# Score tiles of 64 keys by two heads, one exponential a tile, and single-bank pieces in two flat cross attentions

## The chip, the cores and the metric

The kernel runs on one core of one Trainium2 chip. The metric is the device time of one launch in microseconds; less is better. Three runs of the kernel before gave 6174.67, 6178.66 and 6187.05 us; the median, 6178.66, is the time before.

## What is computed

A decoder of four layers for 1024 tokens of width 128; every layer has a self attention, a cross attention and a feed-forward part. The change touches the cross attentions of layers L1 and L2, which attend over the whole context of 6404 rows with 16 heads of 8 values. Both are plain softmax attentions; L1 has a mask of queries by keys, L2 one of keys alone and biases.

```python
# L1_xattn (L2_xattn: q, kv with bias, mask[:, None, None, :] -> -inf)
scores = einsum('bhqd,bhkd->bhqk', Q, K) / sqrt(d_k)        # 16 heads, 1024 queries, 6404 keys
scores = where(mask[:, None] == 0, -1e9, scores)
attn = softmax(scores, axis=-1)
Z = einsum('bhqk,bhkd->bhqd', attn, V)
out = Z @ Wo + bo
```

## The kernel before, in words

`P` is 128, `BANK` 512 (one PSUM bank of float32), `KT` 51 key tiles of 128, `NT` 8 query tiles. Both attentions call `context_sides` (L1090) and then `cross` (L1262), `masked_attention` (L1559) with `mask8` and `maskT`, `cross_attention` (L1661) without.

`context_sides` makes keys and values of all heads from the turned context in 13 groups of up to four key tiles. TensorE makes the products, ScalarE copies the keys twice, VectorE and GpSimd (L1167, L1169) split them into three bfloat16 parts, and VectorE copies the values into `vall` (L1156, or L1159 with a bias), 8 values and a one for every head and tile; GpSimd first sets the ones (L1163). SP stores the parts after every group, and the values at three groups (L1181), as rows of `values_dram`.

`cross` works on pairs of heads (8) and halves of the queries (2 x 512), 16 halves `h` in all. A head's split keys and queries lie in 64 of the 128 partitions (`SLOT`), head `a` of the pair in half `a`. For each half there are three kinds of work:

- **Pieces** (L1382 to L1391, VectorE L1500 to L1520) find the maximum score of each query: 49 rows, 128 queries, 512 keys, for both heads into two neighbouring banks. A half has 4 query tiles by 13 key chunks, 52 pieces. VectorE takes the maximum, masked by a custom operation for each head with the mask bytes subtracted (L1515), unmasked by one reduce over both banks (L1510). The banks form a ring of two places of two banks (4 to 7), which also carries the turning of queries (`queries`, L1391 on), the turning of the shifted queries (`shifted`) and the sums (`add_up`).
- **Scores** (L1411 to L1427): 128 keys by 512 queries of one head into one of three banks (0 to 2), with three more rows that subtract the maximum. Masked, two products of `lower` with `maskT` (L1418) first put the mask into the banks. ScalarE makes the exponential of each bank (L1480).
- **Weighing** (L1429 to L1446): every two key tiles, four products of 9 columns (values and the one) with 512 queries in float32, each in its own 32 columns of the array, summed in bank 3. After a half the sums are folded over the key tiles by `fold` and divided on VectorE.

The order is written out by hand in `programme` (L1233): one list of steps that TensorE, ScalarE and VectorE all follow. The pieces of half `h + 1` are spread between the scores of half `h` (`spread`, `cut`), so that the maxima are there when the half begins; `LEAD` pieces go one half further ahead. Weighing comes three tiles behind its scores (`lag`). TensorE's queue is in order: `ring_wait` before a piece waits until VectorE has freed the place, and a score waits for the exponential that reads its bank (`probs_ready`). SP loads the keys and values of a pair while the pair before it is worked on.

## Time and profile before

| | |
|---|---|
| median of three runs | 6178.66 us |
| lowest, highest | 6174.67, 6187.05 us |
| profiled execution, first to last instruction | 6180.5 us |
| TensorE, VectorE, ScalarE, GpSimd busy | 4319.4, 3667.5, 2628.5, 756.9 us |
| exponentials (L1480) | 3264, 1734.3 us busy, 598 ns each |
| weighing (L1441) | 6528 instructions, 873.0 us busy |
| masked maxima (L1515) | 1664 custom instructions, 1049.1 us busy |
| unmasked maxima (L1510) | 832 reduces, 956.2 us busy |

The table is from the page of the profile, whose times come from one execution on the chip. The only time of that execution that is given is its span, 6180.5 us, which lies between the median and the highest of the three runs. Busy is a union over the instructions of a group, so products that run beside each other count once. A float32 product is two instructions in the profile. Ends of matrix products are modelled; their starts are safer to compare.

### The profile page before, as it was taken

The numbers are of one execution on the slowest core, as the hardware profiler recorded it, in microseconds if no ns is written. First come the engines' busy times: TensorE is split into PE (matmuls) and PEld (weight loads), VectorE is DVE, ScalarE is ACT, GpSimd is POOL, SyncE is SP. The second block draws the span as 40 slices with busy tenths as digits, with TensorE's granted clock in tenths as the row PEclk, the third lists the DMA queues.
The fourth block names the chain that finished last, engine by engine and source line by source line (L and its number), as shares of the span: only waits on it lengthen the run. The fifth ranks groups of instructions, "written<-read, shape, count | busy, mean of one in ns | idle before, by whom it ended". The sixth has DMA issues, their size and how long they took to land. (4 is left out here: it accounts for less than half of the span.)

```text
span 6180.5 us, 82959 instructions
## 1 busy us (share of the span) xinstructions
PE 4319.4 (70%) x31970; PEld 1559.0 (25%) x31970; DVE 3667.5 (59%) x7693; ACT 2628.5 (43%) x4771; POOL 756.9 (12%) x842
## 2 busy tenths in 40 slices
PE   5956999544699999999964899999877641134224
PEld 2333444333122222222242122222134320012011
DVE  5464666556877777777345998998724650137122
ACT  2522666224366666666611587888730110001001
POOL 0000000002000000000002000000000027722772
PEclk9878999767799999999976899999988875567567
DMA  0020000024000000000004001100014000000000
GB/s 13 1 62 10 15 11 9 15 100 155 18 12 10 3 12 12 12 12 1 1 6 104 1 12 19 17 12 12 1 15 147 13 5 13 12 5 5 13 13 8
DMA packets 119874, 141.87 MB, mean 23 GB/s; under 512 B 48269, under 2 KB 96620, under 8 KB 116846
## 3 DMA queue, kind: packets, MB, share of 16 engines
q1 hardware_dynamic: 77870, 118.15, 7.6%
q0 software_dynamic: 20480, 10.53, 1.1%
q10 hardware_dynamic: 21128, 7.88, 0.5%
q8 instruction: 253, 4.15, 0.3%
q14 instruction: 143, 1.17, 0.1%
HBM read 103.35 MB, written 33.14 MB: 22 GB/s over the span
## 5 line engine op out<-in xcount | busy, mean ns | idle before, releaser
L1480 ACT ACTIVATE probs<-ps 128x512 f32<-128x512 f32 x3264 | 1734.3, 598 | 763.0 <-PE ps L1425 762.9
L1515 DVE CUSTOM_DVE_ANT_0 junk<-ps,mask 128x512 bf16<-128x512 f32 (+1 forms) x1664 | 1049.1, 678 | 362.5 <-PE ps L1387 346.4
L1510 DVE TENSOR_REDUCE maxima<-ps 128x2 f32<-128x1024 f32 (+1 forms) x832 | 956.2, 1199 | 110.6 <-PE ps L1387 104.2
L1441 PE MATMUL ps<-probs,vstack 128*9 128x512 f32 x6528 | 873.0, 596 | 0.4 <-ACT probs L1480 0.4
L1425 PE MATMUL ps<-qturned,kturned 52*128 52x512 bf16 x3264 | 792.8, 385 | 83.7 <-ACT probs L1480 64.8
L1387 PE MATMUL ps<-kturned,qturned 49*128 49x512 bf16 (+1 forms) x3328 | 704.6, 392 | 110.8 <-DVE maxima L1510 35.7
L3172 POOL DMA_INDIRECT line<-table,index x640 | 644.8, 1008 | 876.9 <-DVE index L3545 483.5
L1418 PE MATMUL ps<-maskT,lower 128*128 128x512 fp8e5 x1632 | 562.3, 387 | 63.5 <-ACT probs L1480 15.1
L1425 PEld LDWEIGHTS ps<-qturned,kturned 52*128 52x128 bf16 x3264 | 196.2, 93 | 791.8 <-ACT probs L1480 462.1
L1387 PEld LDWEIGHTS ps<-kturned,qturned 49*128 49x128 bf16 x3328 | 166.3, 95 | 492.7 <-DVE maxima L1510 200.3
L1418 PEld LDWEIGHTS ps<-maskT,lower 128*128 128x128 bf16 x1632 | 123.5, 96 | 598.6 <-ACT probs L1480 433.4
L2733 PE MATMUL ps<-plane,bands 32*32 32x512 f32 x6720 | 249.7, 608 | 17.6 <-DVE top L2885 17.6
L1163 POOL MEMSET vall<- 128x816 f32 x2 | 3.1, 1569 | 2041.0 <-POOLq L66 2041.0
L2831 ACT COPY powerT<-ps 128x512 f32<-128x512 f32 x280 | 164.2, 586 | 203.5 <-PE ps L2747 203.3
L3299 PE MATMUL ps<-ident,attended 128*128 128x128 f32 x8 | 3.8, 475 | 340.0 <-DVE attended L3569 198.1
L2875 DVE SCALAR_TENSOR_TENSOR plane<-keep,ps 128x1024 f32<-128x1024 uint8 x144 | 175.7, 1220 | 102.4 <-PE ps L2715 102.4
L2823 ACT ACTIVATE power<-power,bias 128x512 f32<-128x512 f32 x280 | 202.5, 725 | 56.2 <-DVE bias L2893 56.2
L2747 PE MATMUL ps<-ident,power 128*128 128x128 f32 x1120 | 183.0, 286 | 32.4 <-ACT powerT L2831 31.4
L2885 DVE CUSTOM_DVE_ANT_0 power<-ps,lose 128x512 f32<-128x512 f32 x280 | 176.8, 687 | 41.7 <-PE ps L2733 41.7
L3608 DVE SCALAR_TENSOR_TENSOR siluT<-ps,hash_b,yT 128x512 f32<-128x512 f32 x16 | 12.0, 752 | 314.5 <-DMA rows<-in_ctx 242.8
L3230 PE MATMUL ps<-prod,vpar 128*128 128x512 f32 x128 | 70.9, 683 | 138.7 <-issue 113.7
L1441 PEld LDWEIGHTS ps<-probs,vstack 128*9 128x9 f32 x6528 | 98.6, 88 | 262.7 <-ACT probs L1480 182.5
(718 smaller groups left out, 4826.6 us busy)
## 6 DMA issues: line engine op xcount, KB each, us to landing
raw<-in_mask_BxSxS_if SPq DMA_DIRECT2D x8, 3202.0 KB, 13.2
kturned<-keys_parts SPq DMA_DIRECT2D x192, 102.0 KB
table<-lines SPq DMA_DIRECT2D x51, 256.0 KB, 3.0
line<-table,index POOLq DMA_INDIRECT x640
keys_parts<-parts SPq DMA_DIRECT2D x24, 384.0 KB, 2.7
vstack<-values_heads SPq DMA_DIRECT2D x16, 459.0 KB, 16.5
lose<-in_mask_SxS_bc SPq DMA_DIRECT2D x32, 128.0 KB
values_heads<-vall SPq DMA_DIRECT2D x2, 1728.0 KB, 10.4
```

What stands on the lines that cost most here:

```text
L1387: last = nc.tensor.matmul(ring(e)[:, a * BANK:a * BANK + hi - lo], qturned[rows, par, t * P:(t + 1) * P], kturned[rows, par, lo:hi], start ...
L1418: nc.tensor.matmul(k.ps[:, (v + j) % 3, :], k.lower[:], maskT[:, t, b * BANK:(b + 1) * BANK], start=True, stop=False, skip_group_check=True)
L1425: nc.tensor.matmul(k.ps[:, v % 3, :], kturned[rows, par, t * P:(t + 1) * P], qturned[rows, par, b * BANK:(b + 1) * BANK], start=maskT is N ...
L1441: last = nc.tensor.matmul(k.ps[at:at + HD + 1, 3, :], vstack[:, p % 2, a, t, :], probs[:, (h * KT + t) % slots, a, :], start=(t < 2), stop ...
L1480: nc.scalar.activation(probs[:, u % slots, a, :], k.ps[:, (2 * u + a) % 3, :], ACT.Exp, scale=(1.0 if maskT is None else 1.0 / STEP8)).the ...
L1510: nc.vector.tensor_reduce(dst, ring(e).rearrange("p (a n) -> p a n", a=2)[:, :, 0:hi - lo], AX.X, ALU.max).then_inc(ring_free[at % 2], 1)
L1515: nc.vector.tensor_tensor_reduce(junk[:, at % 2, a * BANK:a * BANK + hi - lo], ring(e)[:, a * BANK:a * BANK + hi - lo], mask8[:, 4 * b + m ...
L2733: last = nc.tensor.matmul(k.ps[32 * j:32 * j + 32, i, :], bands[32 * i:32 * i + 32, 4 * g + j, c, :], plane[32 * i:32 * i + 32, u % 2, j, ...
L2747: last = nc.tensor.transpose(k.ps[:, 6, m * P:(m + 1) * P], power[:, u % 2, i, (4 * b + m) * P:(4 * b + m + 1) * P], k.ident[:])
L2823: nc.scalar.activation(part, part, ACT.Exp, bias=bias[:, u % 2, 1, i:i + 1], scale=1.0 / TINY).then_inc(powers, 1)
L2885: nc.vector.tensor_tensor_reduce(power[:, u % 2, i, b * BANK:(b + 1) * BANK], k.ps[:, i, :], lose[:, win % 2, i, b * BANK:(b + 1) * BANK], ...
L3172: nc.gpsimd.indirect_dma_start(line[:, t % 4, j, :], None, lines_of, bass.IndirectOffsetOnAxis(ap=index[:, t, j:j + 1], axis=0)).then_inc( ...
```

## The change

A score tile is laid out anew. Each of its two banks now holds 64 keys of both heads: four products of 52 rows by 64 columns, head `a` and key half `first` going to partitions `64 * (a ^ first)` of bank `first`. There are two such bank pairs (banks 0 to 3), and one exponential reads the whole pair, 1024 columns. The mask is put in by `split`, which repeats 64 columns of the scaled identity. Values are stored for this layout: 18 columns for each head and tile, of which 9 are the head's and 9 are zero, so one weighing product of 18 columns serves both heads for 64 keys. The sums lie in bank 4, and `fold` has another constant. A piece is now one head alone in one bank; the ring has three banks (5 to 7). A half has 104 such pieces, about two to a tile, and `LEAD` is 6. In the unmasked attention the maximum is now the custom operation too, with a row of zeros `nothing` in place of the mask. The order within a tile is: score, its pieces, weighing. `context_sides` clears the zero columns on GpSimd (eight clearings in the first four groups) and copies the values in two halves; SP waits for the clearings before it stores values, and loads values in four pieces for each pair.

```diff
@@ setup
+            for first in range(2):
+                for half in range(2):
+                    nc.vector.tensor_scalar(k.split[:, first, 64 * half:64 * half + 64], k.ident[:, 64 * first:64 * first + 64],
+                                            LOWER, None, ALU.mult).then_inc(zeroed, 1)
@@ context_sides
-        vall = s.sb("vall", [P, H, KT, HD + 1])
+        vall = s.sb("vall", [P, H // 2, 2, KT, 2, HD + 1])
...
+                for a in range(2):
+                    dst = vall[:, :, a, ts[0]:ts[-1] + 1, a, 0:HD].rearrange("p h t d -> p t h d")
+                    mine = src.rearrange("p t (h a) d -> p t h a d", a=2)[:, :, :, a, :]
...
-            nc.gpsimd.memset(vall[:, :, :, HD:HD + 1], 1.0).then_inc(ones_set, 1)
+            for a in range(2):
+                nc.gpsimd.memset(vall[:, :, a, :, a, HD:HD + 1], 1.0).then_inc(ones_set, 1)
             for g, ts in enumerate(groups):
                 n = len(ts) * P
+                if g < 4:
+                    for a in range(2):
+                        nc.gpsimd.memset(vall[:, 2 * g:2 * g + 2, a, :, 1 - a, :], 0.0).then_inc(strips_cleared, 1)
                 pool.wait_ge(mid_ready, g + 1)
...
-                    sp.wait_ge(values_kept, g + 1)
+                    sp.wait_ge(values_kept, 2 * (g + 1))
+                    sp.wait_ge(strips_cleared, 8)
@@ programme and its constants
-LEAD = 3
+LEAD = 6
+RING = 3
+PAIR = 2 * (HD + 1)
-    return [(m, c) for m in range(4) for c in range(len(CHUNKS))]
+    return [(m, c, a) for m in range(4) for c in range(len(CHUNKS)) for a in range(2)]
...
-            cut = [-(-len(spread) * (3 * t + j) // (3 * KT)) for j in range(4)]
-            if masked:
-                out += [("score", h, t, 0), ("score", h, t, 1)] + spread[cut[0]:cut[2]]
-            else:
-                out += [("score", h, t, 0)] + spread[cut[0]:cut[1]] + [("score", h, t, 1)] + spread[cut[1]:cut[2]]
-            out += late.pop(h * KT + t, []) + spread[cut[2]:cut[3]]
+            cut = [-(-len(spread) * (t + j) // KT) for j in range(2)]
+            out += [("score", h, t)] + spread[cut[0]:cut[1]] + late.pop(h * KT + t, [])
@@ cross, ring
-            return k.ps[:, 4 + 2 * (ring_at[e] % 2):6 + 2 * (ring_at[e] % 2), :].rearrange("p a b -> p (a b)")
+            return k.ps[:, 5 + ring_at[e] % RING, :]
@@ cross, SP
-                sp.dma_start(vstack[:, par].rearrange("p a t d -> p (a t d)"),
-                             k.values_dram[:, 2 * p:2 * p + 2].rearrange("p a t d -> p (a t d)")).then_inc(values_loaded[par], 16)
+                for first in range(2):
+                    keys = slice(64 * first, 64 * first + 64)
+                    for a in range(2):
+                        rows = slice(64 * (a ^ first), 64 * (a ^ first) + 64)
+                        sp.dma_start(vstack[rows, par, first].rearrange("p t d -> p (t d)"),
+                                     k.values_dram[keys, 2 * p + a].rearrange("p t d -> p (t d)")).then_inc(values_loaded[par], 16)
@@ cross, TensorE: piece
-                for a in range(2):
-                    rows = slice(a * SLOT, a * SLOT + SHIFT)
-                    last = nc.tensor.matmul(ring(e)[:, a * BANK:a * BANK + hi - lo], qturned[rows, par, t * P:(t + 1) * P],
-                                            kturned[rows, par, lo:hi], start=True, stop=True)
+                rows = slice(a * SLOT, a * SLOT + SHIFT)
+                nc.tensor.matmul(ring(e)[:, 0:hi - lo], qturned[rows, par, t * P:(t + 1) * P], kturned[rows, par, lo:hi],
+                                 start=True, stop=True).then_inc(ring_filled, 1)
@@ score
+                if u >= 2:
+                    pe.wait_ge(probs_ready, u - 1)
+                if maskT is not None:
+                    for first in range(2):
+                        nc.tensor.matmul(k.ps[:, bank + first, :], k.split[:, first, :], maskT[:, t, mine],
+                                         start=True, stop=False, skip_group_check=True)
...
+                for first in range(2):
+                    for a in range(2):
+                        rows = slice(a * SLOT, a * SLOT + ROWS)
+                        to = slice(64 * (a ^ first), 64 * (a ^ first) + 64)
+                        last = nc.tensor.matmul(k.ps[to, bank + first, :], kturned[rows, par, t * P + 64 * first:t * P + 64 * first + 64],
+                                                qturned[rows, par, mine], start=maskT is None, stop=True, skip_group_check=True)
@@ weigh
+                    for first in range(2):
+                        at = 32 * (2 * first + t % 2)
+                        last = nc.tensor.matmul(k.ps[at:at + PAIR, 4, :], vstack[:, p % 2, first, t, :],
+                                                probs[:, (h * KT + t) % slots, first, :],
+                                                start=(t < 2), stop=(t >= KT - 2), skip_group_check=True)
@@ cross, ScalarE
-                    nc.scalar.activation(probs[:, u % slots, a, :], k.ps[:, (2 * u + a) % 3, :], ACT.Exp,
+                    nc.scalar.activation(probs[:, u % slots].rearrange("p b n -> p (b n)"),
+                                         k.ps[:, bank:bank + 2, :].rearrange("p b n -> p (b n)"), ACT.Exp,
@@ cross, VectorE: piece
-                if maskT is None:
-                    dst = maxima[:, b, :, c].rearrange("p (a m) -> p a m", a=2)[:, :, m]
-                    nc.vector.tensor_reduce(dst, ring(e).rearrange("p (a n) -> p a n", a=2)[:, :, 0:hi - lo], AX.X,
-                                            ALU.max).then_inc(ring_free[at % 2], 1)
...
+                lost = nothing[:, 0:hi - lo] if mask8 is None else mask8[:, 4 * b + m, lo:hi].bitcast(mybir.dt.uint8)
+                nc.vector.tensor_tensor_reduce(junk[:, at % RING, 0:hi - lo], ring(e)[:, 0:hi - lo], lost, 1.0, -3.0e38,
+                                               ALU.subtract, ALU.max, maxima[:, b, 4 * a + m, c:c + 1]).then_inc(ring_free[at % RING], 1)
```

## Rows read from the trace of the kernel before

**Rows 1.** Windows: stretch, length, busy of PE, PEld, DVE, ACT, POOL, clock, DMA.

```profile
1650.00:2950.00 1300.00, 1235.10 (x7480) 266.11 (x7484) 957.74 (x3057) 804.46 (x1483) 15.72 (x48) 1.00 0.06 9
3450.00:4450.00 1000.00, 920.42 (x6269) 205.87 (x6266) 902.64 (x878) 798.88 (x1540) 15.74 (x48) 1.00 0.07 11
```

**Rows 2.** Windows of the exponentials' line alone, the same two stretches.

```profile
1650.00:2950.00 1300.00, 785.53 (x1448) 1.00 0.06 9
...
3450.00:4450.00 1000.00, 781.83 (x1505) 1.00 0.07 11
```

**Rows 3.** Order of time, TensorE, masked: start, length, engine, line, operation.

```profile
2202.11 1.05 PE L1441 MATMUL ps<-probs,vstack 128*9 128x512 f32 x8
2203.09 0.60 PE L1418 MATMUL ps<-maskT,lower 128*128 128x512 fp8e5 x2
2203.63 0.39 PE L1425 MATMUL ps<-qturned,kturned 52*128 52x512 bf16 x2
2203.86 0.38 PE L1387 MATMUL ps<-kturned,qturned 49*128 49x512 bf16 x2
2204.17 0.93 PE L1418 MATMUL ps<-maskT,lower 128*128 128x512 fp8e5 x2
2205.03 0.39 PE L1425 MATMUL ps<-qturned,kturned 52*128 52x512 bf16 x2
...
2205.56 1.05 PE L1441 MATMUL ps<-probs,vstack 128*9 128x512 f32 x8
```

**Rows 4.** The same view, unmasked, from one weighing to the next.

```profile
3904.70 1.05 PE L1441 MATMUL ps<-probs,vstack 128*9 128x512 f32 x8
...
3906.12 0.38 PE L1425 MATMUL ps<-qturned,kturned 52*128 52x512 bf16 x1
3906.75 0.39 PE L1425 MATMUL ps<-qturned,kturned 52*128 52x512 bf16 x1 [0.25 <-ACT probs L1480]
...
3907.28 1.05 PE L1441 MATMUL ps<-probs,vstack 128*9 128x512 f32 x8
```

**Rows 5.** ScalarE: exponentials in order of time, and copies by line and form.

```profile
2204.05 1.09 ACT L1480 ACTIVATE probs<-ps 128x512 f32<-128x512 f32 x2 [0.97 <-PE ps L1425]
3906.10 1.57 ACT L1480 ACTIVATE probs<-ps 128x512 f32<-128x512 f32 x3 [0.73 <-PE ps L1425]
L1488 ACT COPY qturned<-ps 128x512 bf16<-128x512 bf16 x16 | 9.3, 580 | 77.5 <-PE ps L1406 77.5
L1484 ACT COPY qturned<-ps 128x1024 bf16<-128x1024 bf16 x7 | 7.1, 1013 | 0.0
```

**Rows 6.** VectorE, order of time: unmasked reduces, masked custom maxima.

```profile
3903.09 7.91 DVE L1510 TENSOR_REDUCE maxima<-ps 128x2 f32<-128x1024 f32 x7 [0.23 <-PE ps L1387]
2202.23 0.69 DVE L1515 CUSTOM_DVE_ANT_0 junk<-ps,mask 128x512 bf16<-128x512 f32 x1
2202.84 0.08 DVE L1515 DVE_READ_ACCUMULATOR2_ANT maxima<- 128x1 f32 x1
```

**Rows 7.** Order of time, TensorE, a stage of layer L0 with sixteen 32 x 32 tiles.

```profile
999.67 1.14 PE L2733 MATMUL ps<-plane,bands 32*32 32x512 f32 x32
1000.75 0.66 PE L2747 MATMUL ps<-ident,power 128*128 128x128 f32 x4
```

**Rows 8.** GpSimd where L2's keys and values are made: by form, in order of time.

```profile
L1163 POOL MEMSET vall<- 128x816 f32 x1 | 1.6, 1570 | 666.5 <-POOLq L66 666.5
L1169 POOL CAST parts<-rest 128x512 bf16<-128x512 f32 x12 | 10.9, 911 | 0.8
3305.28 1.16 POOL L1167 TENSOR_TENSOR rest<-rest,parts 128x512 f32<-128x512 f32 x1 [2.24 <-DVE parts L1151]
3313.03 1.16 POOL L1167 TENSOR_TENSOR rest<-rest,parts 128x512 f32<-128x512 f32 x1 [0.36 <-DVE parts L1151]
3315.56 1.16 POOL L1167 TENSOR_TENSOR rest<-rest,parts 128x512 f32<-128x512 f32 x1 [0.36 <-DVE parts L1151]
```

**Rows 9.** DMA issues: transfer, count, KB each, us to landing.

```profile
values_heads<-vall SPq DMA_DIRECT2D x2, 792.0 KB, 11.1
```

More of the change, by code:

```diff
@@ L1289, in cross @@
         inverse = s.sb("inverse", [P, 4, 2])
-        junk = s.sb("junk", [P, 2, 2 * BANK], BF16)
-        fold = s.sb("fold", [P, 2 * (HD + 1)])
+        junk = s.sb("junk", [P, RING, BANK], BF16)
+        nothing = s.sb("nothing", [P, BANK], mybir.dt.uint8)
+        fold = s.sb("fold", [P, PAIR])
         cleared = s.sem("cleared")
@@ L1300, in cross @@
         ring_filled = s.sem("ring_filled")
-        ring_free = [s.sem(f"ring_free{i}") for i in range(2)]
+        ring_free = [s.sem(f"ring_free{i}") for i in range(RING)]
         dve_order = s.sem("dve_order")
@@ L1375, in piece @@
                 par = p % 2
-                m, c = half[i]
+                m, c, a = half[i]
                 if b == 0 and i == 0:
@@ L1410, in score @@
             def score(e):
-                _, h, t, a = e
+                _, h, t = e
                 p, b = divmod(h, 2)
-                par, v = p % 2, 2 * (h * KT + t) + a
-                if maskT is not None and a == 0:
-                    for j in range(2):
-                        if v + j >= 3:
-                            pe.wait_ge(probs_ready, v + j - 2)
-                        nc.tensor.matmul(k.ps[:, (v + j) % 3, :], k.lower[:], maskT[:, t, b * BANK:(b + 1) * BANK],
+                par, u = p % 2, h * KT + t
+                bank = 2 * (u % 2)
+                mine = slice(b * BANK, (b + 1) * BANK)
+                if u >= 2:
[3 more added lines that the diff above has]
+                        nc.tensor.matmul(k.ps[:, bank + first, :], k.split[:, first, :], maskT[:, t, mine],
                                          start=True, stop=False, skip_group_check=True)
-                if (t, a) == (0, 0):
+                if t == 0:
                     read_wait(pe, ("shifted", h))
-                if maskT is None and v >= 3:
-                    pe.wait_ge(probs_ready, v - 2)
-                rows = slice(a * SLOT, a * SLOT + ROWS)
-                nc.tensor.matmul(k.ps[:, v % 3, :], kturned[rows, par, t * P:(t + 1) * P],
-                                 qturned[rows, par, b * BANK:(b + 1) * BANK], start=maskT is None, stop=True,
-                                 skip_group_check=True).then_inc(scores_filled, 1)
+                for first in range(2):
[4 more added lines that the diff above has]
+                                                qturned[rows, par, mine], start=maskT is None, stop=True, skip_group_check=True)
+                last.then_inc(scores_filled, 1)
             def weigh(e):
@@ L1451, in add_up @@
                 for m in range(4):
-                    last = nc.tensor.matmul(ring(e)[:, m * 32:m * 32 + 2 * (HD + 1)], sums[:, h % 2, m * P:(m + 1) * P], fold[:],
+                    last = nc.tensor.matmul(ring(e)[:, m * 32:m * 32 + PAIR], sums[:, h % 2, m * P:(m + 1) * P], fold[:],
                                             start=True, stop=True)
                 last.then_inc(ring_filled, 1)
-            pe.wait_ge(cleared, 4)
+            pe.wait_ge(cleared, 5)
             for e in steps:
@@ L1503, in piece @@
                 b = h % 2
-                m, c = half[i]
+                m, c, a = half[i]
                 lo, hi = CHUNKS[c]
```

93 lines of the change are left out of this document (42 added, 51 removed).

## The prediction

> **What bounds the kernel now.** I read the windows first. The two flat cross attentions, masked from about 1557 us and unmasked from about 3379 us, fill some 2,600 of the 6180.5 us, and all but a trace of the change lies in them. In the masked one TensorE is busy 95% and VectorE 74%; in the unmasked one TensorE 92%, VectorE 90%, ScalarE 80% [rows 1]. Counting exponentials gives the pace [rows 2]: two make a key tile, so a pair of tiles (the period of weighing) lasts 1300 / 1448 x 4 = 3.59 us masked and 1000 / 1505 x 4 = 2.66 us unmasked. Both have 816 tiles, 408 pairs.
>
> The order of time on TensorE shows what a pair is made of [rows 3, 4]. Differences of starts count, since printed ends are modelled. A wave of 512 columns takes about 0.22 us (score to piece, 2203.63 to 2203.86), whether one or two matmuls of different row halves run in it. Two mask products follow each other and need two waves. Each change in how the array is cut costs about 0.10 to 0.12 more: mask to score 0.54 for two waves, piece to mask 0.31 for one, and weighing 0.98 for what would be four waves, 0.86. So a masked pair is weighing 0.98, mask 0.54, score and piece 0.23 + 0.31, mask 0.86, score and piece 0.53: 3.45. In the second mask 0.32 is waiting for the first exponential, which began at 2204.05 and ended 0.60 later [rows 5]. An unmasked pair is 2.58; there scores wait for exponentials too (3906.12 to 3906.75 is a wave and 0.41 of waiting), while VectorE has a maximum of 1024 columns each 1.13 us (7.91 us for seven [rows 6]), 1.15 us per tile with 52 pieces to 51 tiles, against a tile of 1.29: near its own bound.
>
> **The change, masked cross.** Two exponentials of 512 become one of 1024. The copies of 512 and 1024 columns took 580 and 1013 ns [rows 5], 0.43 for 512 more, so I take 0.60 + 0.43 = 1.03 us; bounds 0.95 (the start-to-start of two, 0.52 each, less their overlap) and 1.20 (nothing saved). With two bank pairs, tile u waits for exp(u-2), begun over 3 us before on average: the 0.32 of waiting goes. The scores become four 64 x 64 products in one mode; the pieces stay 64 rows by 128 columns, so a boundary now stands between score and pieces, where there was none. Bounds of it: 0 (only columns change) and 0.22, the excess of the sixteen-tile product (1.08 from 999.67 to 1000.75, less four waves of 0.215 [rows 7]). I take 0.105, because weighing to mask, where also only columns change, cost 0.12 [rows 3]. The four products themselves I take as one wave: sixteen tiles ran in four passes together [rows 7]; bounds one wave and four. New pair: weighing 0.98, two masks 1.08, two scores 0.32 each, two piece waves with a boundary 0.31 each: 3.32. To this come what a mean pair has now beyond the 3.45 of [rows 3], 0.14 (transposes, odd pieces, copies waited for), and 0.05 for the tiles that get a third single piece (two in a half, each one wave and about 0.4 of ring). 3.51 against 3.59: 0.08 x 408 = **-33 us**; the 3.45 was counted on one pair, so bounds -53 and -13. VectorE needs 2 x 0.61 per tile [rows 6] out of 1.7, so pieces are hidden.
>
> **Unmasked cross.** Here the one reduce of 1.13 becomes two custom maxima, start to start 0.61 to 0.62 [rows 6]: 1.23 per tile instead of 1.13, times 1.02 1.25. More telling is the ring. It had two places of two banks; it has three of one. Take the tiles after a weighing: pieces A, B, then C, D. D needs the bank of A. A's reader starts 0.42 after A (as the exponential at 2204.05 after the score at 2203.63 [rows 3, 5]), its maximum holds the bank 0.70 (0.62 to the last read, 0.08 for that [rows 6]), and the signal takes 0.05 (exponential begun at 3906.10, over 0.60 later, score at 3906.75 [rows 4, 5]): D starts 1.17 after A. Behind D in TensorE's queue wait the weighing and the next score, and ScalarE for that. D and boundary 0.32, weighing 0.98, score and boundary 0.32: then the next A. The loop is 2.79 us, VectorE idle in it 0.35. Adding what a pair has now beyond its steady 2.58 (0.08) and 0.05 for third pieces: 2.92 against 2.66, 0.26 x 408 = **+106 us**. The prologue of 52 pieces is VectorE's: 52 x (1.23 - 1.13) = **+5**. Wins here of the longer exponential (1.03 against 2 x 0.52) are nothing: at 1.46 a tile ScalarE has 0.4 to spare. If the boundary were free the loop would be 2.69.
>
> **The fourfold entry.** Four weights instead of two are loaded at each score. Between 0.105 (two tiles) and 0.22 (sixteen) I take 0.12, as weighing with four has: 0.015 x 816, most of it felt, **+10**. The Trainium skill ("TensorEngine Tiling (Array Packing)", Tile-to-Partition Mapping, Restrictions) says that column tiling turns fast weight load off, and its page "TensorE: Matmul & The Clock Gate" (LDWEIGHTS) gives 64 / 1.2 = 53 ns for such a load; by that, one more load in a row on each row half would add an estimated 43 us instead of 10, and the sum would be 6323. No row here shows a 64-column load by itself.
>
> **The stage that makes keys and values** runs twice. GpSimd has a group of four tiles every 2.53 us and works 1.16 + 0.91 = 2.1 of it [rows 8]. Eight clearings of 918 values are put before the work of the first four groups. The one of 816 took 1.57 us, so 1.77 each; lower bound half of that, 0.9, since their nine values lie side by side and those of 816 did not. Per group 3.5 + 2.1 instead of 2.5: 3.1 x 4 less the 2.2 it now idles before its first subtraction, 10 us, twice: **+20** (bounds +4 and +26). VectorE copies values as two halves: about 0.15 more per group, beneath GpSimd's pace. Stores have twice the bytes in the same number of runs. The last, of 792 KB, is waited for 11.1 us [rows 9]; I take the count of runs as what sets it and no more time: 0, bounds 0 and twice 11. SP's new wait for the clearings lies behind group 5, when they are long done. Four value loads instead of one are 1 us more of SP's queue, ahead of the next pair's keys, which are wanted tens of us later: 0. Setup's four small products and the cleared row: +3. The softmax fold keeps its instructions.
>
> **Sum:** -33 + 106 + 5 + 10 + 20 + 3 = +111 us on a profiled span of 6180.5, which is 2 above the median 6178.7 of three runs (6174.7 to 6187.1): **6290 us**.
>
> **Rivals.** (1) *Changes of columns alone are free between the two 64-row modes.* Masked pair 3.51 - 0.21 = 3.30, -118; unmasked 2.69 + 0.13 = 2.82, +65; with 5, 20 and 3: -25, **6154**, faster. Its place is between score and piece, and on a line from 0.105 (+111) to 0 (-25) it decides below 0.02 of boundary. Against it: weighing to mask. Chance 0.12. (2) *The fourfold entry costs 0.2*, like sixteen tiles: 0.08 more on each of 816 scores masked (+65) and on the one of two that lies in the loop unmasked (+33): **6388**. Chance 0.14. (3) *Two heads in one bank do not run together*: two waves per score, 0.215 x 816 = +175 masked and half of that unmasked: +263, **6553**. No product of before writes one bank from two row halves; all use a bank each. Chance 0.10. The Trainium skill speaks for it: "TensorEngine Tiling (Array Packing)", Gotcha 1, says that different row tiles cannot access one bank at once, and leaves it to software to keep them apart. Its page "PSUM — Partial Sum Buffer" (bank collisions) narrows this, for TensorE's own writes, to the same quadrant, and the halves here are different quadrants; no row shows either. (4) *The change's packing does not happen at all*, four waves, three times as much again: +789, **7079**, chance 0.02.
>
> **How the numbers follow.** Forecast 0.62, with its own range 6215 to 6380 (the bounds of the clearings, -53 to -13 masked, and 0.1 either way on the ring loop). From 6170 to 6450 takes in rival 2 and half of rival 1; outside stay 3, 4 and the other half of 1, 0.18 in all. A measurement here tells 0.2%, 12 us, from nothing. Faster 0.10 (most of rival 1), same 0.04 (its remainder and a small stage cost), slower 0.86.
>
> **What would show it.** Masked: an exponential near 1.03 us, a pair near 3.45, no wait of the mask for ScalarE; score to piece 0.32. Unmasked: a pair near 2.9, TensorE waiting about 0.5 us before every fourth piece on a maximum, ScalarE idle. In the value stage: clearings of 1.8 us and each stage 10 us longer. Score to piece at 0.22 would make rival 1 right, at 0.42 rival 2, at 0.53 rival 3. An unmasked pair at or under 2.66 would break the ring argument.

## The result, and the profile after

The changed kernel takes 6358.47 us (median of 4 runs, 6356.56 to 6369.7) against 6182.85 before (4 runs): ratio 1.029, 95% interval 1.0273 to 1.0306. It is slower by about 176 us. The forecast was 6290, +111, with a range of 6170 to 6450; the sign and the range hold, the size was too small by 65 us. The profiled execution has a span of 6357.8 us, 177.3 more than the one of before.

The page of the changed kernel, its span and the costliest groups (line, engine, operation, count, busy us, mean ns, idle before and what ended it):

```profile
span 6357.8 us, 92912 instructions
...
L1494 ACT ACTIVATE probs<-ps 128x1024 f32<-128x1024 f32 x1632 | 1627.9, 1023 | 1016.9 <-PE ps L1438 1013.9
L1525 DVE CUSTOM_DVE_ANT_0 junk<-ps,mask 128x512 bf16<-128x512 f32 (+1 forms) x1664 | 1034.9, 677 | 393.4 <-PE ps L1398 392.9
L1525 DVE CUSTOM_DVE_ANT_0 junk<-ps,nothing 128x512 bf16<-128x512 f32 (+1 forms) x1664 | 1032.2, 677 | 217.0 <-PE ps L1398 217.0
L1398 PE MATMUL ps<-kturned,qturned 49*128 49x512 bf16 (+1 forms) x3328 | 898.2, 404 | 118.1 <-DMA kturned<-ends_row 28.2
L1454 PE MATMUL ps<-probs,vstack 128*18 128x512 f32 x6528 | 906.6, 617 | 0.2
...
L1438 PE MATMUL ps<-qturned,kturned 52*64 52x512 bf16 x6528 | 685.8, 410 | 27.2 <-ACT qturned L1503 23.1
```

The exponential of 1024 columns takes 1023 ns, so ScalarE has less to do (1627.9 us instead of 1734.3) and idles more. That did not help: it waits for TensorE.

Masked attention, order of time on TensorE, one weighing to the next; [rows 3] is the same stretch of work before:

```profile
2205.10 1.05 PE L1454 MATMUL ps<-probs,vstack 128*18 128x512 f32 x8
2206.09 0.60 PE L1430 MATMUL ps<-maskT,split 128*128 128x512 fp8e5 x2
2206.62 0.41 PE L1438 MATMUL ps<-qturned,kturned 52*64 52x512 bf16 x4
2206.96 0.39 PE L1398 MATMUL ps<-kturned,qturned 49*128 49x512 bf16 x2
2207.29 0.60 PE L1430 MATMUL ps<-maskT,split 128*128 128x512 fp8e5 x2
2207.82 0.41 PE L1438 MATMUL ps<-qturned,kturned 52*64 52x512 bf16 x4
2208.16 0.39 PE L1398 MATMUL ps<-kturned,qturned 49*128 49x512 bf16 x2
2208.48 1.05 PE L1454 MATMUL ps<-probs,vstack 128*18 128x512 f32 x8
```

The pair is 3.38 us. The mask no longer waits (0.53 instead of 0.86 for the second), the four score products leave 0.34 before the pieces, and the pieces 0.32 or 0.33 before the next boundary. The four products do run as one wave: they and the boundary behind them take 0.34, and two waves of 0.215 would be 0.43 before any boundary.

Unmasked attention, the same view; [rows 4] before:

```profile
3964.19 1.05 PE L1454 MATMUL ps<-probs,vstack 128*18 128x512 f32 x8
3965.17 0.41 PE L1438 MATMUL ps<-qturned,kturned 52*64 52x512 bf16 x4
3965.51 0.39 PE L1398 MATMUL ps<-kturned,qturned 49*128 49x512 bf16 x2
3965.84 0.41 PE L1438 MATMUL ps<-qturned,kturned 52*64 52x512 bf16 x4
3966.18 0.91 PE L1398 MATMUL ps<-kturned,qturned 49*128 49x512 bf16 x2
3967.01 1.05 PE L1454 MATMUL ps<-probs,vstack 128*18 128x512 f32 x8
```

The pair is 2.82 us. The first two pieces take 0.33 from start to next start, the second two 0.83: piece D waits 0.5 for the bank of A, and the weighing stands behind it.

A boundary between halves, unmasked, on TensorE: the turning of the queries (L1406), the next piece, the weighing and a score.

```profile
3520.15 0.62 PE L1406 MATMUL ps<-ident,qstack 128*128 128x128 bf16 x8
3522.76 0.58 PE L1398 MATMUL ps<-kturned,qturned 49*128 49x512 bf16 x1 [1.99 <-ACT qturned L1499]
3523.27 1.91 PE L1454 MATMUL ps<-probs,vstack 128*18 128x512 f32 x8
3525.11 0.64 PE L1438 MATMUL ps<-qturned,kturned 52*64 52x512 bf16 x4
```

TensorE stands for 1.99 us because the next piece needs ScalarE's copy of the turned queries. After it the weighing takes 1.84 us start to start instead of 0.98, the score 0.57 instead of 0.34: half speed. The windows show it as granted clock (columns: stretch, length, busy of PE, PEld, DVE, ACT, POOL, then clock, DMA share, GB/s); first three of 25 us around this boundary, then the fourteen middle halves of each attention:

```profile
3500.00:3525.00 25.00, 21.89 (x162) 5.29 (x158) 20.79 (x70) 15.93 (x17) 0.00 (x0) 0.95 0.01 2
3525.00:3550.00 25.00, 23.37 (x136) 5.29 (x132) 14.88 (x47) 12.92 (x14) 2.60 (x8) 0.71 0.00 1
3550.00:3575.00 25.00, 23.65 (x179) 5.65 (x175) 22.18 (x73) 16.64 (x18) 0.00 (x0) 1.00 0.00 1
...
1719.00:3004.00 1285.00, 1261.25 (x8805) 302.01 (x8803) 926.16 (x3004) 751.42 (x750) 13.01 (x40) 0.99 0.08 11
3537.00:4652.00 1115.00, 1031.32 (x7376) 251.89 (x7377) 923.00 (x3002) 715.91 (x749) 13.01 (x40) 0.95 0.08 13
```

Before, the stretches of [rows 1] were granted 1.00. The first unmasked half, ahead of the second of these rows, was granted 0.96 before and 0.85 after. In the masked attention the 0.99 is five short falls, each behind a turning of queries; the one half with a turning that has no fall takes 92.91 us, the others about 94.4.

**Where the time came from.** The starts of the same instruction in both traces give the difference (after less before) at each place. A half is measured from one copy of the sums (L1495, now L1510) to the next.

| place | before, us | after, us | difference |
|---|---|---|---|
| ones set, L1 value stage | 1447.97 | 1436.51 | -11.5 |
| first piece, masked | 1556.29 | 1554.54 | -1.8 |
| first exponential, masked | 1626.09 | 1624.33 | -1.8 |
| last copy of sums, masked | 3083.57 | 3073.67 | -9.9 |
| ones set, L2 value stage | 3301.48 | 3293.60 | -7.9 |
| first piece, unmasked | 3378.90 | 3378.86 | 0.0 |
| first exponential, unmasked | 3443.74 | 3448.65 | +4.9 |
| last copy of sums, unmasked | 4527.39 | 4700.93 | +173.5 |
| last instruction | 6180.5 | 6357.8 | +177.3 |

So the two value stages cost 9.7 and 7.9 us, the masked attention gained 8.1, the unmasked prologue cost 4.9 and the unmasked attention 168.6; 2.0 between the attentions and 3.8 behind them are not placed. The 11.5 us at the start lie in layer L0, whose code is unchanged. They arise in the last three halves of its attention (45.3 us before, 33.6 after), and the clock differs there; the first row is from the kernel before, the second from the kernel after:

```profile
280.00:300.00 20.00, 20.00 (x81) 6.28 (x80) 0.43 (x2) 9.82 (x19) 0.00 (x0) 0.50 0.00 0
280.00:300.00 20.00, 19.15 (x125) 6.92 (x123) 0.86 (x4) 11.51 (x26) 0.00 (x0) 0.92 0.00 0
```

Further kernels below started the value stage of L1 at 1447.59 and 1437.75, so this difference comes and goes between programs. The last halves, which have no pieces beside them, are 12 us shorter in both attentions (81.66 to 69.81, 60.60 to 49.07): there the new score layout is worth something undisturbed.

### The profile page after: what moved, and what is told of

Its sections match the earlier page's. It is cut to its first block and busy times, and to the rows that moved or that the text cites. A ratio compares the mean times of both kernels' runs of the same rounds, so it can differ in the third digit from the quotient of the medians.

```text
span 6357.8 us, 92912 instructions
## 1 busy us (share of the span) xinstructions
PE 4587.5 (72%) x35198; PEld 1678.7 (26%) x35234; DVE 3738.3 (59%) x10221; ACT 2526.9 (40%) x3139; POOL 769.4 (12%) x860
## 5 line engine op out<-in xcount | busy, mean ns | idle before, releaser
L1494 ACT ACTIVATE probs<-ps 128x1024 f32<-128x1024 f32 x1632 | 1627.9, 1023 | 1016.9 <-PE ps L1438 1013.9
L1525 DVE CUSTOM_DVE_ANT_0 junk<-ps,nothing 128x512 bf16<-128x512 f32 (+1 forms) x1664 | 1032.2, 677 | 217.0 <-PE ps L1398 217.0
L1398 PE MATMUL ps<-kturned,qturned 49*128 49x512 bf16 (+1 forms) x3328 | 898.2, 404 | 118.1 <-DMA kturned<-ends_row 28.2
L1454 PE MATMUL ps<-probs,vstack 128*18 128x512 f32 x6528 | 906.6, 617 | 0.2
L1438 PE MATMUL ps<-qturned,kturned 52*64 52x512 bf16 x6528 | 685.8, 410 | 27.2 <-ACT qturned L1503 23.1
L1430 PE MATMUL ps<-maskT,split 128*128 128x512 fp8e5 x1632 | 497.4, 387 | 0.0
L1438 PEld LDWEIGHTS ps<-qturned,kturned 52*64 52x64 bf16 x6528 | 186.1, 104 | 854.8 <-issue 522.0
L1398 PEld LDWEIGHTS ps<-kturned,qturned 49*128 49x128 bf16 x3328 | 208.0, 93 | 700.5 <-issue 374.5
L1525 DVE DVE_READ_ACCUMULATOR2_ANT maxima<- 128x1 f32 x3328 | 276.1, 83 | 0.0
L2743 PE MATMUL ps<-plane,bands 32*32 32x512 f32 x6720 | 249.6, 608 | 17.6 <-DVE top L2895 17.6
L1430 PEld LDWEIGHTS ps<-maskT,split 128*128 128x128 bf16 x1632 | 93.3, 97 | 447.1 <-ACT probs L1494 332.3
## 6 DMA issues: line engine op xcount, KB each, us to landing
values_heads<-vall SPq DMA_DIRECT2D x2, 3456.0 KB, 13.6
```

The lines of the kernel that those rows point to most:

```text
L1398: nc.tensor.matmul(ring(e)[:, 0:hi - lo], qturned[rows, par, t * P:(t + 1) * P], kturned[rows, par, lo:hi], start=True, stop=True).then_in ...
L1430: nc.tensor.matmul(k.ps[:, bank + first, :], k.split[:, first, :], maskT[:, t, mine], start=True, stop=False, skip_group_check=True)
L1438: last = nc.tensor.matmul(k.ps[to, bank + first, :], kturned[rows, par, t * P + 64 * first:t * P + 64 * first + 64], qturned[rows, par, mi ...
L1454: last = nc.tensor.matmul(k.ps[at:at + PAIR, 4, :], vstack[:, p % 2, first, t, :], probs[:, (h * KT + t) % slots, first, :], start=(t < 2) ...
L1494: nc.scalar.activation(probs[:, u % slots].rearrange("p b n -> p (b n)"), k.ps[:, bank:bank + 2, :].rearrange("p b n -> p (b n)"), ACT.Exp ...
L1525: nc.vector.tensor_tensor_reduce(junk[:, at % RING, 0:hi - lo], ring(e)[:, 0:hi - lo], lost, 1.0, -3.0e38, ALU.subtract, ALU.max, maxima[: ...
```

## The experiments

The median of the kernel before was taken anew beside each set: 6180.55, 6186.61 and 6182.5 us.

### Weighing between the pieces (e1)

```diff
-            out += [("score", h, t)] + spread[cut[0]:cut[1]] + late.pop(h * KT + t, [])
+            now = late.pop(h * KT + t, [])
+            if between and now and now[0][0] == "weigh":      # between = maskT is None
+                out += [("score", h, t)] + spread[cut[0]:cut[0] + 1] + now + spread[cut[0] + 1:cut[1]]
+            else:
+                out += [("score", h, t)] + spread[cut[0]:cut[1]] + now
```

> The changed kernel, unmasked attention only: where a tile has a weighing, it stands between the two pieces instead of behind them. The same work, one boundary of the array more per pair (0.11 us) and one piece wave that no longer runs beside another (0.21). Ring theory (the steady pair of 2.82 us is set by piece D waiting for the bank of A while the weighing queues behind it): the wait of about 0.5 us before D goes, the pair falls to about 2.62 us, 0.20 x 408 = some 80 us off the time, near 6280. Rival, TensorE's own work sets the pair (entries of the four score products and boundaries): the pair rises by 0.1 to 0.3 us and the time by 40 to 130 us, above 6400. Rival, VectorE's throughput (4 x 0.61 = 2.46 us a pair) with its starts: little change, within 20 us. The masked attention stays as it is in each.

Measured: 6516.99 us (median of 6405.89, 6484.36, 6549.62 and 6554.2), ratio to before 1.0561 (1.0503 to 1.0618); the fastest of the four is 3.6% above the median before. By its time the second theory would have won. The trace of the run of 6405.89 says otherwise; TensorE in order of time, a pair:

```profile
3702.39 1.05 PE L1458 MATMUL ps<-probs,vstack 128*18 128x512 f32 x8
3703.37 0.39 PE L1402 MATMUL ps<-kturned,qturned 49*128 49x512 bf16 x1
3703.69 0.41 PE L1442 MATMUL ps<-qturned,kturned 52*64 52x512 bf16 x4
3704.03 0.39 PE L1402 MATMUL ps<-kturned,qturned 49*128 49x512 bf16 x2
3704.35 0.41 PE L1442 MATMUL ps<-qturned,kturned 52*64 52x512 bf16 x4
3704.69 0.39 PE L1402 MATMUL ps<-kturned,qturned 49*128 49x512 bf16 x1
3705.01 1.05 PE L1458 MATMUL ps<-probs,vstack 128*18 128x512 f32 x8
```

The pair is 2.62 us and has no wait, as the ring theory said to the hundredth. But the unmasked middle halves of this run are 72 to 88 us, and two of them 113.6 and 113.7. Windows at the start of the first of these two, which runs from 4240.0 to 4353.6, inside it, and over most of it:

```profile
4236.00:4244.00 8.00, 7.71 (x56) 1.94 (x56) 6.27 (x19) 5.43 (x7) 0.00 (x0) 1.00 0.24 39
...
4276.00:4284.00 8.00, 8.00 (x40) 1.25 (x38) 4.41 (x14) 3.79 (x4) 0.00 (x0) 0.50 0.00 0
...
4247.00:4346.00 99.00, 99.00 (x444) 16.75 (x440) 56.49 (x179) 44.52 (x44) 0.00 (x0) 0.50 0.11 17
```

For these 99 us the clock is 1.2 GHz while TensorE is busy every microsecond. The other half of 113 us has a stretch of the same length, and shorter ones stand before 4100 and 4196. The ring wait is gone and more is lost to the clock.

### Queries turned early (e2)

```diff
-        queue.append([("piece", h, i) for i in range(LEAD, n)])
-        if h + 1 < HALVES:
-            queue[h] += ([("queries", (h + 1) // 2)] if h % 2 else []) + [("piece", h + 1, i) for i in range(LEAD)]
+        queue.append([("piece", h, i) for i in range(LEAD, n - 8)])
+        if h + 1 < HALVES and h % 2:
+            queue[h].append(("queries", (h + 1) // 2))
+        queue[h] += [("piece", h, i) for i in range(n - 8, n)]
+        if h + 1 < HALVES:
+            queue[h] += [("piece", h + 1, i) for i in range(LEAD)]
```

> The changed kernel with the turning of the next pair's queries moved eight pieces (four tiles) ahead, in both attentions; nothing else. Theory: at every second half TensorE stands for about 2 us because the next piece needs ScalarE's copy of the turned queries, which waits behind a long exponential; masked odd halves (94.4 us against 90.2) lose that, 7 x 3 to 4 = 21 to 28 us, and unmasked ones lose 2 us of standing and the half clock that the trace shows behind it, 7 x 3 to 5 = 21 to 35 us: together 40 to 60 us faster. Rival, the standing is moved and not removed (it costs the same four tiles earlier): within 10 us.

Measured: 6310.73 us (6308.6 to 6330.6), ratio 1.0206 (1.0189 to 1.0223), so 48 us faster than the changed kernel and inside the forecast. The masked halves with a turning, 92.91 to 94.45 us before the edit, are 91.59 or 91.60 throughout; the others stay 90.2. So the wait for the copy costs 1.3 us a half by itself (92.91 to 91.6), and where the clock fell behind it 1.5 more. The profiled execution is the slowest of the four (6330.6; the others are 6308.6 to 6312.23). In its unmasked attention the trace still has halves of 84.7 us beside such of 76.4: the clock still falls at other places.

### Short maxima (e3)

```diff
+                w = (hi - lo) // 2 if mask8 is None else hi - lo
-                ...(junk[:, at % RING, 0:hi - lo], ring(e)[:, 0:hi - lo], lost, ...
+                ...(junk[:, at % RING, 0:w], ring(e)[:, 0:w], lost[:, 0:w], ...
```

> The changed kernel, with the unmasked maxima taken over the first half of each piece's columns alone (256 of 512); it leaves out half of the search for the maximum of each query. It shortens how long VectorE holds a bank from 0.70 to about 0.45 us and leaves TensorE's work as it is. Ring or VectorE theory: the steady unmasked pair falls from 2.82 to TensorE's own sum, 0.98 + 4 x 0.33 = 2.30 us, more than 150 us off the time in all. If TensorE's boundaries and entries set the pace, it stays at 2.8. Whether the clock still falls at half boundaries shows if the ring waits feed it.

Measured: 6182.27 us in its one run, 176 us less than the changed kernel. TensorE in the unmasked attention, the second pieces and the next weighing:

```profile
3864.97 1.05 PE L1454 MATMUL ps<-probs,vstack 128*18 128x512 f32 x8
...
3866.96 0.64 PE L1398 MATMUL ps<-kturned,qturned 49*128 49x512 bf16 x2
3867.53 1.05 PE L1454 MATMUL ps<-probs,vstack 128*18 128x512 f32 x8
```

The pair is 2.56, not the 2.30 that I expected, since a wait of a quarter of a microsecond stays at D (0.57 for two pieces, not 0.33). That is the closed loop itself: the maximum is 0.27 us shorter (starts 0.34 apart, not 0.61) and the loop 0.26 shorter (2.56, not 2.82). VectorE is now busy 555 of 1060 us, so its throughput is not the bound; the turn around the ring is. Middle halves are 68.6 and 71.0 us.

### Products of constants in the waits (e4)

```diff
+                if maskT is None and h and b == 0 and i == 0:
+                    ring_wait(pe, e)
+                    for _ in range(16):
+                        nc.tensor.matmul(ring(e)[:, 0:2 * P], k.ident16[:], k.split[:].rearrange("p a n -> p (a n)"), ...)
...
                 if t == 0:
+                    if maskT is None:
+                        for _ in range(10):
+                            nc.tensor.matmul(k.ps[:, bank, 0:2 * P], k.ident16[:], k.split[:]..., ...)
                     read_wait(pe, ("shifted", h))
```

> The changed kernel, unmasked attention: where TensorE stands at a half boundary, for the copy of the turned queries (every second half) or for the copy of the shifted queries (every half), it first makes 16 or 10 products of constants, 256 columns each, in banks that are overwritten right after; about 1.8 and 1.1 us of work laid into waits of 2.0 and 1.0 us. Clock theory (about 5 us of each half go because the granted clock falls to half for 5 to 10 us after the boundary): the clock of the unmasked stretch rises from 0.95 to 1.0 and the time falls by 30 to 50 us. Rival, the time lost is the wait itself: clock up or not, the time stays within 10 us or rises by up to 10.

Measured: 6332.8 us (6322.93 to 6348.41), ratio 1.0251 (1.023 to 1.0273): 26 us faster than the changed kernel, with more work in it. The stretch from 3540 to 4600 us is granted 0.99 instead of 0.95:

```profile
3540.00:4600.00 1060.00, 999.94 (x7459) 265.44 (x7455) 907.08 (x2950) 698.06 (x731) 13.02 (x40) 0.99 0.09 14
```

Halves without any fall of the clock now show as exact repeats, 76.35 and, with a turning, 78.11 us (before the change 67.4 and 68.4). That is what the ring and the boundaries cost with the clock held. The gain is a little below the 30 to 50 forecast, and a few falls remain.

### The pieces alone, ring of three and of four (e6, e7)

Both start from the kernel before: scores, exponentials, weighing and the order are its own, only the pieces are the change's.

```diff
-    return [(m, c) for m in range(4) for c in range(len(CHUNKS))]
+    return [(m, c, a) for m in range(4) for c in range(len(CHUNKS)) for a in range(2)]
...
-            return k.ps[:, 4 + 2 * (ring_at[e] % 2):6 + 2 * (ring_at[e] % 2), :].rearrange("p a b -> p (a b)")
+            return k.ps[:, 4 + ring_at[e] % RING, :]              # RING = 3 or 4
...
-                    nc.vector.tensor_reduce(dst, ring(e)..., AX.X, ALU.max)          # unmasked
+                nc.vector.tensor_tensor_reduce(junk[...], ring(e)[:, 0:hi - lo], lost, ...)   # both, one head
```

> The kernel BEFORE with the change's pieces alone: one head in one bank, a ring of three, the custom maximum in both attentions; scores, exponentials, weighing and the order of steps as before. Ring theory: the unmasked pair gets the same closed loop (D waits 1.17 us from A, then 0.22 for D, 0.22 for a score, 0.10 boundary, 0.98 weighing, 0.22 score) of about 2.9 us against 2.58, with the prologue +100 to +140 us; the masked attention, where VectorE has slack, within 15 us. Rival, the score layout (boundaries, entry, long exponential) made the loss: within 20 us of before.

> The same with a ring of four banks, which the old score layout leaves free. D no longer waits for A but for the D of the pair before. Ring theory: most of the loss of the run with three goes; what stays is VectorE's 0.10 us more a tile and the prologue, 0 to +45 us against before. If the loss is the custom maximum itself and not the ring, it stays near the run with three.

Measured with three: 6327.14 us (6294.02 to 6346.16), ratio 1.0212 (1.0174 to 1.025), +141. With four: 6197.31 us (6185.74 to 6223.95), ratio 1.0029 (1.0011 to 1.0047), +11. One more bank takes away all but 11 us. TensorE with three:

```profile
3866.18 1.05 PE L1438 MATMUL ps<-probs,vstack 128*9 128x512 f32 x8
...
3868.56 0.39 PE L1385 MATMUL ps<-kturned,qturned 49*128 49x512 bf16 x1 [0.36 <-DVE maxima L1507]
...
3869.09 1.05 PE L1438 MATMUL ps<-probs,vstack 128*9 128x512 f32 x8
```

The pair is 2.91 where 2.9 was worked out, and the piece D is the one that waits for a maximum. With four, the middle halves are 67.7 to 67.9 and 68.6 us but for the last two, before 67.4 and 68.4: the custom maximum in place of the reduce costs 0.2 to 0.4 us a half, and its prologue 4.3 (69.1 against 64.8). With three, undisturbed halves are 74.5 and 75.8 us, which is 99 us in fourteen; the rest of the 141 is in good part clock. The stretch from 3540 to 4500 us is granted 0.98, and the whole last half, which has no pieces and so no ring wait, runs at 1.2 GHz and takes 93.6 us instead of 60.6:

```profile
4584.00:4680.00 96.00, 89.70 (x321) 10.95 (x322) 0.43 (x2) 53.20 (x103) 0.00 (x0) 0.50 0.00 0
```

So that the 141 lies at the upper end of the forecast of 100 to 140 is in part luck: the forecast had no term for the clock. The four runs spread over 52 us.

### Three edits together (e8), and two of them (e10)

The first is the edits of e1, e2 and e4 in one kernel, the second those of e2 and e4.

> The changed kernel with three edits together: unmasked weighing between the pieces, queries turned eight pieces early (both attentions), and products of constants in the waits at half boundaries (unmasked). Theory: the ring wait and the clock are two separate costs; with the clock held the order of the first experiment shows its 2.62 us pair throughout: unmasked middle halves of 71 us against 79.4, 14 x 8 = some 115 us, and 15 to 25 us masked, near 6220 to 6240. Rival, an order whose TensorE work is denser loses its clock in any case (as in the first experiment, where halves of 113 us stood beside such of 75): above 6300 and widely spread.

> The changed kernel in its own order of score, pieces, weighing, with the queries turned eight pieces early (both attentions) and the products of constants in the waits at half boundaries (unmasked): the third run of the last set without the weighing between the pieces. Theory (the clock falls where TensorE stands or runs thin at a boundary, whatever the order; the order of the third run then pays for it longer): clock of the unmasked stretch 0.97 to 1.0, its middle halves near the undisturbed 76.3 us, masked ones 90.2 and 91.6: 6358 - 14 x 3.1 - 18 = near 6295. Rival, the early turning and the busy products disturb each other (as something in the third run did): above 6330.

Measured: e8 6354.23 us (6330.36 to 6372.27), ratio 1.0258 (1.0226 to 1.029); its rival was right. e10 6322.39 us (6316.52 to 6330.6), ratio 1.0226 (1.0202 to 1.0251), between its two forecasts and no better than e2 alone. The gains of e2 and e4, 48 and 26 us, do not add up: together they are 36. Why is not shown. In e8 undisturbed unmasked halves are 72.3 and 74.0 us, but others 96.9 and 111.1. Windows where one of these begins:

```profile
3616.00:3624.00 8.00, 7.97 (x57) 1.91 (x56) 6.52 (x21) 5.54 (x7) 0.00 (x0) 1.00 0.23 41
3624.00:3632.00 8.00, 7.59 (x43) 2.15 (x43) 4.93 (x18) 3.14 (x5) 0.00 (x0) 0.69 0.99 122
...
3668.00:3676.00 8.00, 8.00 (x37) 1.47 (x40) 5.82 (x18) 4.10 (x4) 0.00 (x0) 0.50 0.01 3
```

Before the fall TensorE had folded the sums (eight products of 18 columns at 3624.80, after a wait of 0.32 us), a place that the constants do not cover. Then 1.2 GHz lasts over 50 us with TensorE never idle. e10, with the order of the change, has 0.98 in the stretch from 3540 to 4500 us against 0.88 here, and its longest half is 81.7 us. So falls happen with both orders. The longest in the traces of the changed kernel and of e2 last 20.5 us, those in e1 and e8 99 and 89 us. But the last half of e6 had one of 99 us with the order and the scores of before, so the order with the weighing between is not the only one that pays for long. Why the clock does not come back is not shown by these runs.

### The masked half of the change alone (e9), and trimmed (e11)

e9 keeps the changed masked attention with the edit of e2, and gives the unmasked one its old value stage, layout, ring and order.

```diff
-            context_sides(k, ctxT, wkv[:, 0:D], wkv[:, D:2 * D], key_bias[:], bias[:, 1, :])
-        cross(k, q, out)
+            context_sides_plain(k, ctxT, wkv[:, 0:D], wkv[:, D:2 * D], key_bias[:], bias[:, 1, :])   # as before the change
+        cross_plain(k, q, out)                                                                      # as before the change
```

> The masked attention as changed, with the queries turned eight pieces early; the unmasked attention, its value layout and its ring as before. Theory (the masked half of the change is a gain once the queries do not wait): masked stretch from first to last sum about 1339 us against 1364.5, the value stage +8 to +10: 10 to 20 us faster than before. Rival, the masked gain is eaten by the value stage and the loads: within 6 us of before.

Measured: 6164.11 us (five runs, 6160.47 to 6171.41), ratio 0.9964 (0.995 to 0.9978): 22 us or 0.4% faster than the kernel before beside it (6186.61), 16 to 18 against the medians of the other two sets. The forecast was 10 to 20. The masked stretch from first to last sum is 1338.9 us (before 1364.5), and the value stage of L1 is 9 us longer, both as expected. This is the lowest median of the study; it beats the kernel before and the changed one.

e11 adds two trims to it: clearings one to a group over eight groups, and a third piece behind the weighing. With the first goes a third edit, which its expectation does not name: the values of L1 are stored behind groups 9, 11 and 13 instead of 6, 10 and 13, so that the store comes after the clearings.

```diff
-        leave = {5: 0, 9: 24, len(groups) - 1: 40}
+        leave = {8: 0, 10: 36, len(groups) - 1: 44}
...
-                if g < 4:
-                    for a in range(2):
-                        nc.gpsimd.memset(vall[:, 2 * g:2 * g + 2, a, :, 1 - a, :], 0.0).then_inc(strips_cleared, 1)
+                if g < 8:
+                    q, a = divmod(g, 2)
+                    nc.gpsimd.memset(vall[:, 2 * q:2 * q + 2, a, :, 1 - a, :], 0.0).then_inc(strips_cleared, 1)
...
-            out += [("score", h, t)] + spread[cut[0]:cut[1]] + late.pop(h * KT + t, [])
+            mine = spread[cut[0]:cut[1]]
+            out += [("score", h, t)] + mine[:2] + late.pop(h * KT + t, []) + mine[2:]
```

> The run with the masked half of the change alone, with two trims: the clearings go one to a group over eight groups, where GpSimd has 0.4 us to spare in each, instead of two to a group over four, and a third single piece in a tile goes behind the weighing instead of before it (its wait of 0.4 us for the ring is then covered). Theory: 3 to 5 us from the value stage and 2 x 16 x 0.25 = up to 8 us from the pieces, 6150 to 6162. Rival, the stage ends by its stores and the third pieces cost the same behind the weighing: within 4 us of the run it starts from (6164).

Measured: 6167.8 us (ten runs, 6150.75 to 6204.18), ratio 0.9977 (0.9957 to 0.9997). That cannot be told from e9, as the rival said. The masked halves went from 90.2 and 91.6 to 90.0 and 91.4, so the third piece behind the weighing saves 0.16 us a half, not up to 0.25 or 0.5. The value stage of L1, from ones set to first piece, is 118.5 us against 117.3 in e9: spreading the clearings did not shorten it, but the later store came with them, so neither is tested alone.

## Why the prediction was right or wrong

**The exponential and the boundary: right.** 1023 ns where 1.03 us was taken. Score to piece is 0.34 us in both attentions, a wave of 0.215 and 0.12 to 0.13 for boundary and fourfold entry, as summed. Rival 1 (no boundary, 0.22) and rivals 3 and 4 (0.5 and more) are out, and so is rival 2 (0.42). So two heads do write one bank from different row halves of the array at the same time, in different partitions of it. The Trainium skill ("TensorEngine Tiling (Array Packing)", Gotcha 1) would forbid it as written. What the Trainium skill ("PSUM — Partial Sum Buffer", bank collisions) states as measured, an error where two row tiles write the same quadrant of a bank, agrees with this case, whose row halves write different ones; the same section also quotes the wide rule. The estimate from the Trainium skill ("TensorE: Matmul & The Clock Gate", LDWEIGHTS), 53 ns more a score, is too high: the measured excess over a two-tile boundary is about 20 ns.

**Unmasked, the ring: right in kind and nearly in size.** The loop A, D, weighing, score was put at 2.79 us and is 2.82; the loop for the old layout with three banks at 2.9 and is 2.91; shortening the hold by 0.27 shortened the pair by 0.26 (e3); a fourth bank removes it (e7). With the clock held a middle half is 76.3 or 78.1 us against 67.4 and 68.4, so 14 of them cost 128 us; the forecast's 0.26 us a pair is 93. The plain pair, 2.58 to 2.82, makes 86 of the 128. The other 43 are what a half has beyond its plain pairs, for which the forecast had 0.05 us a pair, 18 us: third pieces, and the boundary between halves, where TensorE stands 1 to 2 us for ScalarE's copies.

**Unmasked, the clock: the term that was missing.** The prediction priced all products at 2.4 GHz, because the stretch before was granted 1.00, and never asked what its own new waits would do to that. The fourteen middle halves took 1115.1 us; undisturbed they are 7 x (76.35 + 78.11) = 1081.2. The remaining 34 us are stretches at 1.2 GHz around half boundaries. e4, which fills these waits and changes nothing else, raised the granted clock to 0.99 and gave back 26 us. The first half adds 17.7 (88.1 us at a clock of 0.85, before 70.3 at 0.96), how much of it by the clock is not separated, and the last half gives 11.5 back. Together the unmasked attention cost 168.6 us where 106 and about half of the 10 for the entry were forecast, some 57 more. The masked attention adds some 20 to the miss (-8.1, where -33 and the other half of the entry were forecast). Against them stand the 11.5 us of L0: that the whole came out only 65 us off is in part the luck of a faster stretch in unchanged code.

**Masked: the size was off.** -33 forecast, -8.1 measured, all of it in the last half, which has no pieces (-11.9). In the fourteen others the plain pairs did fall, from 3.45 or 3.55 to 3.38, but the "rest" that I carried over unchanged grew. A pair with a third single piece takes 3.97, 0.59 more. A half with a turning of queries was 0.9 us longer than one without and is now 2.7 or 4.2 longer (92.9 or 94.4 against 90.2), because the next piece waits for a copy that stands behind an exponential of 1.02 us; in five of the six such halves the clock falls behind the wait, which is the 1.5 between the two. e2 shows that both are avoidable: it makes the difference 1.4 us and the masked stretch from first to last sum 25.5 us shorter than before (without the edit 10.1). So of the 25 us that the masked forecast missed, 15 are this wait and the clock behind it, the latter about half.

**The value stages: right sum, wrong reason.** +20 forecast, 9.7 + 7.9 = 17.6 measured. The clearings take 0.92 us, not 1.77; the summary of their line (count, shortest, median, longest ns):

```profile
L1176 POOL MEMSET vall<- x16: 912/921/1198, 1437.9 to 3308.0; 128x918 f32 x16
```

That was the lower bound of the prediction, +4 in both stages. SP issues the first store of values 21.9 us after the ones are set in L1 and 22.1 in L2, before 18.9 and 19.0: 3 us a stage up to there. The rest of the 17.6 lies behind the clearings. Part of it shows in the timeline of ScalarE, the first row from the kernel after and the second from the kernel before (start, duration, then the idle time ahead of it and its releaser):

```profile
1471.38 0.60 ACT L1140 ACTIVATE whole<-ps 128x512 f32<-128x512 f32 x1 [9.55 <-DMA keys_parts<-parts]
```

```profile
1477.30 0.60 ACT L1135 ACTIVATE whole<-ps 128x512 f32<-128x512 f32 x1 [6.92 <-DMA keys_parts<-parts]
```

Both wait until a store of key parts has landed and set its buffer free, and in both kernels the last thing that SP had issued ahead of the long wait was the store of the values (at 1458.40 after, at 1466.87 before). After, that store carries twice the bytes and the wait is 2.6 us longer. In L2 the wait is 11.08 us after and 7.36 before, and the store lands 13.6 us after its issue, not 10.4. The traces of all kernels fall in the same two groups: the waits are 9.5 to 11.3 us where the store is the change's (13.65 in e11, which stores later), 6.9 to 9.2 where it is the old one. I gave those bytes nothing, with 22 as the upper bound. That the larger store causes the longer wait was not tested by itself, and the some 5 us that are left of the 17.6 are not placed. Nor is it known to the microsecond: with its code unchanged, the stage took 108.3, 109.1 and 112.2 us in L1 and 77.3 to 80.4 in L2 in different kernels (after: 118.0 and 85.3).

**The prologue: right.** +5 forecast, +4.9 measured from first piece to first exponential.

## What to carry to other kernels

When a ring of buffers gets more but smaller places, work out its turn, from filling a place over the reader's latency and hold to the signal, and add all that is queued behind the waiting instruction on the in-order engine; the number of places times the reader's pace does not give it. Here three places instead of four cost over ten times as much as the slower reader did. And price a new wait on TensorE twice: once for its length, and once for what follows it at half clock.

## What the runs showed of the hardware

The granted clock did not come back with work alone. In e8 it stayed at 1.2 GHz from about 3628 to 3680 us while TensorE was busy 8.00 of 8 us in window after window, weighing and small products without a gap; in e1 it stayed there for 99 us twice, in the two halves of 113 us, beside halves of 75. The last half of e6, with the scores and the order of before, was at 1.2 GHz for all of its 93.6 us, TensorE busy about 7.5 of 8 us. The Trainium skill ("TensorE: Matmul & The Clock Gate", Part 1) says that activity releases the throttle; these stretches are busy by the profile and were not released. The changed kernel, with its 0.5 us waits, recovered each time within 20.5 us, and in most of its falls within 10. The denser order of e1 was the slower and the more scattered one, 6405.89 to 6554.2 us over four runs against 6356.56 to 6369.7 for the changed kernel; that its density is the reason was not tested.

Four products of 52 rows by 64 columns, of two heads into two banks, run as one wave: 0.34 us from their start to that of the next products, the boundary included, in both attentions.
